# Four graph layers with GpSimd gathers: TensorE does a step's sum before its node stages

## The chip, the cores and the metric

The kernel runs on one core of one Trainium2 chip. The metric is the device time of one execution in microseconds. Three runs of the kernel before gave a median of 9930.19 us (9926.19 to 9943.86). One further execution, the profiled one, took 9929.83 us.

## What is computed

12,500 nodes with 64 features and 200,000 edges, sorted by their target node, go through four residual graph layers, each followed by a layer norm. The edges are the same in all. Cut to what matters:

```
x = layernorm(x + mlp_elu(x + segment_sum(x[src], dst)))
x = layernorm(x + mlp(concat(x, segment_sum(mlp(concat(x[src], x[dst], edge)), dst))))
h = l2norm(mean(x[src]) @ Wl1 + b1 + x @ Wr1);  h = relu(batchnorm(h))
x = layernorm(x + l2norm(l2norm(mean(h[src]) @ Wl2 + b2 + h @ Wr2) + x))
x = layernorm(x + segment_sum(x[src] @ Wrel[edge_type], dst))
```

## The kernel before, in words

The kernel makes five passes over the edges, numbered p = 0 to 4 and called **layers** here: the third reference layer needs two. Each pass gathers, for every edge, one row of a table in HBM (in_x, far_tab, x_tab, h_tab, rel_tab, lines 436 and following). All tables but the first are written by the pass before.

**Edges.** 128 edges are a chunk, 8 chunks a *step* (SUPERS = 196 steps a pass, indexed s). GpSimd issues one indirect DMA a chunk into G, which has 4 slots (s % 4); it may fill a slot again when `summed` says that the sum of step s - 4 is done. 200,000 edges are 1563 chunks (FILLED), so step 195 issues only 3. VectorE builds one-hot matrices OH of the targets (L748), TensorE multiplies each chunk's rows with them into PAG, a window of 96 nodes (`sum_straight`, `sum_window`, 8 matmuls, each of which stands as two records in the trace), and VectorE adds PAG to AGG (L779, `add_straight`). PAG is a single buffer: sum s waits for the add of sum s - 1. VectorE does the add of sum s - 1 in step s, ahead of its one-hot and its stages. In layer 1 the gathered rows are first added to PH, which TensorE computes for the next step (`pre_straight`), with a ReLU on ScalarE; in layer 3 VectorE *shifts* the gathered rows (L977) and ScalarE does the ReLU (L617) before the sum.

**Nodes.** 250 nodes are a *unit* (50 of them, 0 to 49). As soon as the sorted edges of a unit are summed, its dense part is done in four *stages*, 0 to 3 (node0 to node4 on each engine). `straight_schedule` fixes in which step each stage runs; SCHEDULE[s] lists them, mostly one stage in a step, and LATE holds those after the last step. At the end, SCHEDULE[192] is stage 3 of unit 47, 193 to 195 are stages 0, 1 and 2 of unit 48, and LATE is stage 3 of unit 48 and all of unit 49. Twice in a layer the schedule moves closer to the edges: step 104 holds stage 3 of unit 24 and stage 0 of unit 25, step 105 stages 1 and 2 of unit 25, and likewise steps 162 and 163 with units 39 and 40.

Stage 0 is ScalarE's fetch alone (Z, IU, XU, in layer 3 POS too; clearing AGG). What TensorE, VectorE (V) and ScalarE (S) do in the others:

| layer | stage 1 | stage 2 | stage 3 |
|---|---|---|---|
| 0 | T: NA, NB; V: NEG; S: exp; V: NEG | T: NB; V: layer norm (S: root) | T: transpose; S: XT; T: NA; S: STG, stores |
| 1 | T: transpose; S: XT | T: NA; S: POS | T: NB; V: layer norm; S: store |
| 2 | T: transpose; S: XT | T: NA, NB; S: Y; V: norm | T: transpose; S: store, HT; V: statistics |
| 3 | T: NB, NA; S: Y; V: norm | V: norm, layer norm (S: roots) | T: transpose; S: XT; T: PH, 4 products; S: STG, stores |
| 4 | T: transpose | V: layer norm | S: store |

Each engine has its own written-out program (`straight`), and each executes in order. ScalarE's and VectorE's programs for a step are, in this order: ScalarE its ReLU (layers 1 and 3), then its stages; VectorE the add of the last step, the mix or shift (layers 1 and 3), the one-hot for the next step, then its stages. The change touches TensorE's only. A second program (`turns`) is taken when the edge list is not regular enough; for these inputs the written-out one runs.

```
def gathers(p, s):
    ...
    if p == 1:
        pool.wait_ge(mixed, s + 1)
    else:
        pool.wait_ge(summed, SUPERS * p + s + 1)
```

```
if p == 3:
    pool.wait_ge(stored[2], all_stored(2))
```

The second fragment stands at the start of a pass on GpSimd (with its own number in each): no gather of a pass is issued before the last row of its table is stored.

Of the kernel before, what the change touches and what calls it, by code (L numbers as in the profile page):

```python
# [80 lines left out]
def gnn_kernel(nc, x, xT, src_c, dst_c, dst_r, type_c, efT, W1, b1, W2, b2, mW1, mb1, mW2T, mb2,  # L81
               uW1, ub1, uW2, ub2, Wl1, Wr1, sb1, gamma, beta, Wl2, Wr2, sb2, Wrel, out):
    ctx = ExitStack()
    with ctx:
# [253 lines left out]
        def slot_gathered(p, i):  # L338

            return i * (16 * GROUP) + 16 * GROUP * (TURNS * p + 1)  # L340
# [752 lines left out]
        def _(pe):  # L1093
            def mm(dst, lhsT, rhs, start=True, stop=True):
                return nc.tensor.matmul(dst, lhsT, rhs, start=start, stop=stop, skip_group_check=True)  # L1095
# [23 lines left out]
            def sum_window(p, h, m):  # L1119

                msg = HID[:, h % 2, :].rearrange("p (j c) -> p j c", j=GROUP) if p == 1 else G[:, h, :, :]
                for j in range(GROUP):
                    last = mm(PAG[0:m, 0:WIN], msg[:, j, 0:m], OH[:, h % 2, j, :], j == 0, j == GROUP - 1)
                return last
# [44 lines left out]
            def sum_straight(p, s, m):  # L1169

                h = s % SLOTS
                if p == 1:
                    pe.wait_ge(relu_done, s + 1)
                elif p == 3:
                    pe.wait_ge(bn_relu, s + 1)
                else:
                    if p == 0 and s == 0:
                        pe.wait_ge(onehot_ready, 1)
                    pe.wait_ge(added, SUPERS * p + s + 2)
                    pe.wait_ge(gathered[h], slot_gathered(p, s // SLOTS))  # L1180
                sum_window(p, h, m).then_inc(summed, 1)

            def pre_straight(t):

                b = t % 2
                pe.wait_ge(hotT_ready, t + 1)
                for j in range(GROUP):
                    c = slice(j * P, (j + 1) * P)
                    last = mm(PH[b][:, c], MIXT[:, b, c], MIXW[:, b, :], j % 4 == 0, j % 4 == 3)
                last.then_inc(pre_done, 1)  # L1190
# [63 lines left out]
            def batch_norm_row():  # L1254

                pe.wait_ge(bn_ready, 1)
                mm(NA[:, 0:H], BC[:, 2:3].to_broadcast([P, P]), IDENT[:, :]).then_inc(bn_rows, 1)
# [25 lines left out]
            def straight():  # L1283
                for p in range(LAYERS):
                    m = (D + 1, H, D, H, D)[p]
                    if p == 1:
                        pre_straight(0)
                    for s in range(SUPERS):
                        if p == 1 and s + 1 < SUPERS:
                            pre_straight(s + 1)  # L1290
                        for u, stage in SCHEDULE[s]:
                            node[p](u, stage)
                        sum_straight(p, s, m)
                    for u, stage in LATE:
                        node[p](u, stage)
                    if p == 2:
                        batch_norm_row()
# [21 lines left out]
            with pe.If(regular > 0):  # L1319
                straight()  # L1320
# [49 lines left out]
```

## Time and profile before

| | |
|---|---|
| median of the runs | 9930.19 us |
| the profiled execution | 9929.83 us |
| its span in the trace | 9928.0 us |
| GpSimd (POOL) busy | 7381.4 us, 74% |
| TensorE (PE) busy | 5057.8 us, 51% |
| VectorE (DVE) busy | 2602.1 us, 26% |
| ScalarE (ACT) busy | 1280.8 us, 13% |
| mean granted clock of TensorE | 0.583 |

The span runs from the first to the last instruction. An engine's busy time leaves out waits and the issuing of DMAs; the part of a gather that is issuing on GpSimd appears as "issue" beside it. The clock is a share of 2.4 GHz. In the timeline a row is one instruction, or several alike of one block, with its start and its length; the bracket names the idle time of the engine before it and what ended it.

### The profile page before, as it was taken

What the parts mean: (1) busy time and instruction counts of PE and PEld (TensorE: products, weight loads), DVE (VectorE), ACT (ScalarE), POOL (GpSimd) and SP (SyncE); (2) the same over time, 40 slices, a digit from 0 to 9 for tenths busy, and PEclk for the clock granted to TensorE, in tenths of its full rate; (3) what the DMA queues carried; (4) which work ended last, traced back from release to release, by engine and by line L of the source; (5) the groups of instructions that cost most, each with busy time, mean ns of one, the idle gap of its engine ahead of it and who ended that gap; (6) DMA issues with size and microseconds to landing.
All of it is one profiled execution on the core that took longest, in us unless ns stands there. A gap on an engine that the chain in (4) does not pass through costs nothing.

```text
span 9928.0 us, 68540 instructions
## 1 busy us (share of the span) xinstructions
PE 5057.8 (51%) x23622; PEld 4285.6 (43%) x23623; DVE 2602.1 (26%) x5963; ACT 1280.8 (13%) x2646; POOL 7381.4 (74%) x7823
## 2 busy tenths in 40 slices
PE   4555555566666666344444445666666633323333
PEld 3444444456666666333333334444555422222222
DVE  2222222233444443111111113333333311111111
ACT  1111111111111111000000001222222200000000
POOL 7777777767777777677777777777777667777777
PEclk6555555577777777555555555555555555555555
DMA  3111111133333333111111112222222211111111
GB/s 73 33 33 34 33 33 34 32 88 92 93 93 93 93 93 87 27 30 30 30 30 30 30 29 68 78 78 81 79 79 80 76 29 28 28 28 29 28 28 28
DMA packets 396618, 525.10 MB, mean 53 GB/s; under 512 B 175674, under 2 KB 232868, under 8 KB 396200
## 3 DMA queue, kind: packets, MB, share of 16 engines
q0 software_dynamic: 250080, 359.01, 16.0%
q1 hardware_dynamic: 56929, 81.63, 2.8%
q10 hardware_dynamic: 89255, 80.01, 2.6%
q8 instruction: 189, 3.10, 0.1%
q14 instruction: 165, 1.35, 0.0%
HBM read 442.81 MB, written 77.29 MB: 52 GB/s over the span
## 4 chain that ended last, share of the span: by engine, by line
POOL 74%; issue 25%; PE 1%; DVE 0%; DMA 0%; ACT 0%; ACTq 0%; POOLq 0%; DVEq 0%
POOL G L436 74%; PE PAG L1095 0%; PE NB L1095 0%; PE NA L1095 0%; PE PH L1095 0%; DMA G<-in_x,SRC 0%; DMA near_tab<-STG 0%; DVE FA L715 0%; DMA G<-rel_tab,IDX 0%; DMA h_tab<-STG 0%; ACT L503 0%; DMA G<-far_tab,SRC 0%; DMA G<-h_tab,SRC 0%; DVE HT L1031 0%; DMA G<-x_tab,SRC 0%
## 5 line engine op out<-in xcount | busy, mean ns | idle before, releaser
L1095 PE MATMUL PAG<-OH,G 128*64 128x96 f32 (+2 forms) x12544 | 2369.8, 383 | 3844.0 <-DMA G<-rel_tab,IDX 1370.1
L1095 PEld LDWEIGHTS PAG<-OH,G 128*64 128x64 f32 (+2 forms) x12544 | 2167.4, 253 | 4094.6 <-issue 3623.9
L436 POOL DMA_INDIRECT G<-rel_tab,IDX x1563 | 1474.7, 944 | 525.5 <-issue 525.5
L436 POOL DMA_INDIRECT G<-far_tab,SRC x1563 | 1474.9, 944 | 515.6 <-issue 476.1
L436 POOL DMA_INDIRECT G<-x_tab,SRC x1563 | 1475.5, 944 | 503.3 <-issue 476.0
L436 POOL DMA_INDIRECT G<-h_tab,SRC x1563 | 1475.0, 944 | 498.0 <-issue 475.7
L436 POOL DMA_INDIRECT G<-in_x,SRC x1563 | 1479.0, 946 | 476.1 <-issue 475.2
L779 DVE TENSOR_TENSOR AGG<-AGG,PAG 64x96 f32 (+2 forms) x980 | 245.6, 251 | 5510.9 <-PE PAG L1095 5501.0
L1095 PE MATMUL PAG<-OH,HT 128*128 128x96 f32 x3136 | 652.6, 393 | 630.2 <-ACT HT L614 630.2
L748 DVE TENSOR_TENSOR OH<-CONST,DREL 128x768 f32<-128x768 f32 x981 | 927.9, 946 | 3.7 <-issue 2.7
L1095 PEld LDWEIGHTS PAG<-OH,HT 128*128 128x128 f32 x3136 | 607.3, 297 | 678.0 <-ACT HT L614 677.6
L1095 PE MATMUL PH<-HT 128*128 128x128 f32 x3136 | 573.1, 359 | 17.9 <-DVE HT L817 17.8
L1095 PEld LDWEIGHTS PH<-HT 128*128 128x128 f32 x3136 | 558.1, 276 | 21.8 <-DVE HT L817 21.2
L1095 PE MATMUL PH<-wrel,XT 64*125 64x512 f32 x400 | 359.3, 1076 | 257.0 <-ACT XT L486 257.0
L1031 DVE TENSOR_TENSOR HT<-PH,G 128x1024 f32<-128x1024 f32 x196 | 240.0, 1225 | 753.5 <-DMA G<-far_tab,SRC 737.8
L614 ACT ACTIVATE HT<-HT 128x1024 f32<-128x1024 f32 x196 | 207.1, 1057 | 1608.7 <-DVE HT L1031 1608.7
L617 ACT ACTIVATE G<-G 128x1024 f32<-128x1024 f32 x196 | 207.1, 1056 | 1040.7 <-DVE G L977 1040.7
L977 DVE TENSOR_TENSOR G<-G,CONST 128x1024 f32<-128x1024 f32 x196 | 238.9, 1219 | 315.2 <-DMA G<-h_tab,SRC 314.4
L464 ACT ACTIVATE Z<-AGG 64x250 f32<-64x250 f32 (+2 forms) x250 | 101.5, 406 | 1686.2 <-DVE AGG L779 1610.4
L1095 PEld LDWEIGHTS PH<-wrel,XT 64*125 64x125 f32 x400 | 123.4, 323 | 433.3 <-ACT XT L486 276.1
L481 ACT ACTIVATE SQ<-VE 125x2 f32<-125x2 f32 x350 | 71.1, 203 | 1629.4 <-DVE VE L860 1457.1
L817 DVE SCALAR_TENSOR_TENSOR HT<-HT,FIRST,CONST 96x1024 f32<-96x1024 int16 x196 | 248.6, 1268 | 18.6 <-DMA HT<-near_tab 18.6
(151 smaller groups left out, 3840.1 us busy)
## 6 DMA issues: line engine op xcount, KB each, us to landing
rel_tab<-STG ACTq DMA_DIRECT2D x100, 500.0 KB
HT<-dst_rows SPq DMA_DIRECT2D x196, 192.0 KB
HT<-in_efT SPq DMA_DIRECT2D x196, 128.0 KB
G<-in_x,SRC POOLq DMA_INDIRECT x1563
G<-far_tab,SRC POOLq DMA_INDIRECT x1563
G<-x_tab,SRC POOLq DMA_INDIRECT x1563
G<-h_tab,SRC POOLq DMA_INDIRECT x1563
G<-rel_tab,IDX POOLq DMA_INDIRECT x1563
```

The lines of the kernel that those rows point to most:

```text
L436: pool.indirect_dma_start(out=G[:, h, j, 0:tabs[p].shape[1]], out_offset=None, in_=tabs[p], in_offset=bass.IndirectOffsetOnAxis(ap=numbers ...
L464: return nc.scalar.activation(dst, src_, ACT.Copy)
L481: nc.scalar.activation(SQ[0:HALF, :], VE[0:HALF, :], ACT.Sqrt).then_inc(root_ready[p], 1)
L614: nc.scalar.activation(HID[:, h % 2, :], HID[:, h % 2, :], ACT.Relu).then_inc(relu_done, 1)
L617: nc.scalar.activation(G[:, h, :, :], G[:, h, :, :], ACT.Relu).then_inc(bn_relu, 1)
L748: return nc.vector.tensor_tensor(OH[:, b, :, :], IOTA_P.unsqueeze(1).to_broadcast([P, GROUP, WIN]), d.unsqueeze(2).to_broadcast([P, GROUP, ...
L779: return nc.vector.tensor_tensor(dst, dst, PAG[0:m, 0:WIN], ALU.add)
L817: nc.vector.scalar_tensor_tensor(MIXT[0:WIN, b, :], DROW[:, b, :], FIRST[0:WIN, bass.ds(t, 1)], PIOTA_P[0:WIN, :].to_broadcast([WIN, SUPER ...
L977: nc.vector.tensor_tensor(rows_, rows_, CROW_P.unsqueeze(1).to_broadcast([P, GROUP, H]), ALU.add)\
L1031: nc.vector.tensor_tensor(HID[:, h % 2, :], PH[h % 2][:, :], G[:, h, :, :].rearrange("p j c -> p (j c)"), ALU.add)\
L1095: return nc.tensor.matmul(dst, lhsT, rhs, start=start, stop=stop, skip_group_check=True)
```

## The change

In TensorE's written-out program, the call that sums step s moves ahead of the loop over the stages of step s. Nothing else changes; the programs of VectorE, ScalarE, GpSimd and SyncE are the same instruction by instruction.

```diff
                     for s in range(SUPERS):
                         if p == 1 and s + 1 < SUPERS:
                             pre_straight(s + 1)
+                        sum_straight(p, s, m)
                         for u, stage in SCHEDULE[s]:
                             node[p](u, stage)
-                        sum_straight(p, s, m)
                     for u, stage in LATE:
                         node[p](u, stage)
```

TensorE at the end of layer 0, from stage 1 of unit 48. PAG is a sum, 8 matmuls a step; NA and the NB of ONES and Z are stage 1, the NB of w, NEG and rows stage 2, the NB of IDENT and XS opens stage 3. Before:

```order
L1095 MATMUL NA<-Z,w 128x250
L1095 MATMUL NB<-ONES,Z 125x1
L1095 MATMUL NA<-Z,w 128x250
L1095 MATMUL NB<-ONES,Z 125x1
L1095 MATMUL PAG<-OH,G 65x96 x8
L1095 MATMUL NB<-w,NEG 125x64 x2
L1095 MATMUL NB<-rows,ONES 125x64
L1095 MATMUL NB<-w,NEG 125x64 x2
L1095 MATMUL NB<-rows,ONES 125x64
L1095 MATMUL PAG<-OH,G 65x96 x8
L1095 MATMUL NB<-IDENT,XS 64x125 x2
```

and with the change:

```order
L1095 MATMUL PAG<-OH,G 65x96 x16
L1095 MATMUL NA<-Z,w 128x250
L1095 MATMUL NB<-ONES,Z 125x1
L1095 MATMUL NA<-Z,w 128x250
L1095 MATMUL NB<-ONES,Z 125x1
L1095 MATMUL PAG<-OH,G 65x96 x8
L1095 MATMUL NB<-w,NEG 125x64 x2
L1095 MATMUL NB<-rows,ONES 125x64
L1095 MATMUL NB<-w,NEG 125x64 x2
L1095 MATMUL NB<-rows,ONES 125x64
L1095 MATMUL NB<-IDENT,XS 64x125 x2
```

The sum of step 194 (the second half of the x16) now stands ahead of stage 1, and that of step 195 between stage 1 and stage 2 of the unit, where it stood behind stage 2.

TensorE in layer 3, from the sums before stage 3 of unit 47 to the opening of stage 3 of unit 48. NB of wl and the NA are stage 1, the NB of IDENT and PH are stage 3; stages 0 and 2 have nothing on TensorE. Before:

```order
L1095 MATMUL PAG<-OH,G 128x96 x16
L1095 MATMUL NB<-IDENT,XS 64x125 x2
L1095 MATMUL PH<-wrel,XT 125x512 x4
L1095 MATMUL PAG<-OH,G 128x96 x16
L1095 MATMUL NB<-wl,Z 125x64
L1095 MATMUL NA<-wr,POS 125x64
L1095 MATMUL NA<-rows,ONES 125x64
L1095 MATMUL NB<-wl,Z 125x64
L1095 MATMUL NA<-wr,POS 125x64
L1095 MATMUL NA<-rows,ONES 125x64
L1095 MATMUL PAG<-OH,G 128x96 x16
L1095 MATMUL NB<-IDENT,XS 64x125 x2
```

and with the change:

```order
L1095 MATMUL PAG<-OH,G 128x96 x16
L1095 MATMUL NB<-IDENT,XS 64x125 x2
L1095 MATMUL PH<-wrel,XT 125x512 x4
L1095 MATMUL PAG<-OH,G 128x96 x16
L1095 MATMUL NB<-wl,Z 125x64
L1095 MATMUL NA<-wr,POS 125x64
L1095 MATMUL NA<-rows,ONES 125x64
L1095 MATMUL NB<-wl,Z 125x64
L1095 MATMUL NA<-wr,POS 125x64
L1095 MATMUL NA<-rows,ONES 125x64
L1095 MATMUL PAG<-OH,G 128x96 x8
L1095 MATMUL NB<-IDENT,XS 64x125 x2
```

Before, the first x16 are steps 190 and 191; now they are 191 and 192, so that stage 3 of unit 47 follows the sum of step 192. Stage 1 of unit 48 follows the sum of step 194, which it preceded.

## Rows read from the trace of the kernel before

**Rows 1.** The page: chain that ended last by engine; one layer's gathers.
```profile
POOL 74%; issue 25%; PE 1%; DVE 0%; DMA 0%; ACT 0%; ACTq 0%; POOLq 0%; DVEq 0%
...
L436 POOL DMA_INDIRECT G<-h_tab,SRC x1563 | 1475.0, 944 | 498.0 <-issue 475.7
```

**Rows 2.** The waits of GpSimd (POOL): who for whom, us, times, longest.
```profile
POOL G L436 <- PE PAG L1095: 0.9, 3, 0.3
```

**Rows 3.** Timeline, end of layer 0: start, us, engine, line, operation, idle before.
```profile
1962.75 1.20 PE L1095 MATMUL NA<-Z,w 64*128 64x250 f32 x2
...
1966.12 0.86 DVE L891 TENSOR_SCALAR NEG<-NA,b1c 128x250 f32<-128x250 f32 x2 [2.05 <-PE NB L1095]
...
1969.85 0.68 DVE L903 SCALAR_TENSOR_TENSOR NEG<-NA,POS 128x500 f32<-128x500 f32 x1 [2.33 <-ACT NA L503]
...
1970.02 2.80 PE L1095 MATMUL PAG<-OH,G 128*65 128x96 f32 x16 [3.94 <-DMA G<-in_x,SRC]
...
1972.61 1.00 PE L1095 MATMUL NB<-w,NEG 128*125 128x64 f32 x4
...
1978.52 1.10 PE L1095 MATMUL NB<-IDENT,XS 125*64 125x125 f32 x4
```

**Rows 4.** Timeline, end of layer 1: stages 2 and 3 of unit 49.
```profile
3980.31 1.20 PE L1095 MATMUL NA<-XT,u 65*128 65x250 f32 x2 [0.47 <-ACT XT L486]
...
3982.91 0.68 PE L1095 MATMUL NB<-uw,POS 128*125 128x64 f32 x2 [0.56 <-ACT POS L523]
```

**Rows 5.** Timeline, end of layer 2.
```profile
5936.85 0.95 POOL L436 DMA_INDIRECT G<-x_tab,SRC  x1 [0.30 <-issue]
...
5939.40 2.79 PE L1095 MATMUL PAG<-OH,G 128*64 128x96 f32 x16 [6.35 <-DMA G<-x_tab,SRC]
5940.60 0.94 POOL L436 DMA_INDIRECT G<-x_tab,SRC  x1 [0.30 <-issue]
...
5942.12 0.79 PE L1095 MATMUL NA<-wl,Z 64*125 64x128 f32 x2
```

**Rows 6.** Timeline, end of layer 3: steps 193 to 195 and what follows.
```profile
7906.21 1.21 DVE L977 TENSOR_TENSOR G<-G,CONST 128x1024 f32<-128x1024 f32 x1
...
7907.45 1.06 ACT L617 ACTIVATE G<-G 128x1024 f32<-128x1024 f32 x1 [4.58 <-DVE G L977]
...
7908.56 3.73 PE L1095 MATMUL PAG<-OH,G 128*128 128x96 f32 x16 [2.66 <-ACT G L617]
...
7912.09 0.57 PE L1095 MATMUL NB<-wl,Z 128*125 128x64 f32 x2
...
7912.60 1.22 DVE L977 TENSOR_TENSOR G<-G,CONST 128x1024 f32<-128x1024 f32 x1
...
7915.35 0.52 ACT L557 ACTIVATE Y<-NB,IU 125x64 f32<-125x64 f32 x2 [0.45 <-PE NA L1095]
...
7917.51 0.48 DVE L984 SCALAR_TENSOR_TENSOR Y<-Y,RS,XU 125x64 f32<-125x64 f32 x2
...
7919.28 1.21 DVE L977 TENSOR_TENSOR G<-G,CONST 128x1024 f32<-128x1024 f32 x1
...
7921.28 0.28 DVE L876 TENSOR_TENSOR Y<-Y 125x128 f32<-125x128 f32 x1
...
7921.64 3.73 PE L1095 MATMUL PAG<-OH,G 128*128 128x96 f32 x16 [2.66 <-ACT G L617]
...
7925.30 1.09 PE L1095 MATMUL NB<-IDENT,XS 125*64 125x125 f32 x4
...
7926.92 7.18 PE L1095 MATMUL PH<-wrel,XT 64*125 64x512 f32 x8 [0.53 <-ACT XT L486]
...
7935.08 0.41 ACT L464 ACTIVATE Z<-AGG 128x250 f32<-128x250 f32 x1 [0.35 <-ACT STG L571]
...
7936.23 0.58 ACT L552 ACTIVATE POS<-HT,BSH,BSC 128x250 f32<-128x250 f32 x1
```

**Rows 7.** Windows, end of layer 3: us, busy PE, PEld, DVE, ACT, POOL; PEclk.
```profile
7913.60:7964.00 50.40, 28.90 (x75) 17.53 (x74) 14.02 (x51) 11.49 (x27) 0.94 (x1) 0.50 0.13 43
```

## The prediction

> **What bounds the kernel now.** I read the chain that ended last first: GpSimd's gathers hold 74% of the span and the "issue" time between them 25% [rows 1]. The group of one layer's 1563 gathers says how: 944 ns each and 475.7 us of issue gaps, so (1475.0 + 475.7) / 1563 = 1.248 us per gather and 9.985 us per step of eight. The reader is to see that 5 x 1563 x 1.248 us is 9.75 ms of the 9.93. Then the waits, for whether anything ever holds GpSimd up inside a layer: it waited for a sum (PAG) three times, 0.9 us in all [rows 2]. So TensorE has slack on every step but at a layer's end, where GpSimd may not gather until the last rows of a table are stored; there everything behind the last gather is on the path. Last, the timeline of those four ends and of single steps in layer 3.
>
> Step 195 has only 3 chunks, so its gather takes 3.7 us and not 10, and stage 2 of unit 48 is scheduled in step 195, stage 1 in 194. Those two stages now stand behind the sums of their steps.
>
> **The change, part by part.** No instruction is added or removed, no DMA is moved, and the other engines' orders are the same; TensorE alone exchanges about four blocks in each unit. What changes is who waits. Until now a stage's matmuls ran in the 6 or so us in which TensorE waited for gather s. Now they run after sum s, VectorE's part of the stage comes after them, and VectorE's add of sum s, for which sum s+1 waits (layer 3: the shift of gather s+1), is queued behind that part.
>
> *Layer 0's end* [rows 3]. Before, stage 1 of unit 48 ran at 1962.75, VectorE began on it 3.37 us later and finished at 1969.85 + 0.68, before it mattered. Sum 194 began at 1970.02, stage 2 at 1972.61, and the transpose that opens stage 3 at 1978.52. Now: sum 194 at 1970.02, stage 1 at 1972.6 (+2.6), VectorE at 1976.0 (+3.37), done at 1980.4 (+4.41, two ScalarE passes in it), the add of sum 194 and the handover 0.4 (chosen; adds of 0.25 us stand in all timelines), sum 195 at 1980.8, stage 2 at 1983.4, stage 3 at 1989.3 (the 5.91 us that lay between the two before). That is **+10.8 us**. The 5.91 holds a sum that now comes earlier, so 0.2 to 0.4 of it may go: 10.4 to 10.8.
>
> *Layer 1's end* [rows 4]. VectorE has work in stage 3 only. Stage 2's two products (NA) come behind sum 195 and ScalarE's pass after them is then in the open: from the NA matmul to the matmul of stage 3 it took 2.60 us for unit 49. **+2.6 us**.
>
> *Layer 2's end* [rows 5]. Before, stage 2 began at 5942.12, while the last gather (issued 5940.60) was still under way. A gather issued at 5936.85 let its sum start at 5939.40, 2.55 later; so sum 195 starts at 5943.15 and stage 2 a sum later (5942.12 - 5939.40 = 2.72), at 5945.9: **+3.8 us**.
>
> *Layer 4's end*: stage 2 has no TensorE work, and stage 1 of unit 48 fits between sums 194 and 195 while the last gather lands. **0**.
>
> *Layer 3* [rows 6] is the large one, as its steps were nearly full. In terms of VectorE's shift of a gather (L977), a plain step, shift to shift, takes 7912.60 - 7906.21 = 6.39 us with no gather to wait for: 2.35 to the sum, 4.04 from the sum. Stages 0 and 2 still cost no more than that, stage 2's VectorE part lying beside the sum. Stage 1 now takes 2.35 to the sum, 3.53 to its products (7912.09 - 7908.56), 3.26 until ScalarE's scaling (7915.35), 2.64 until VectorE ends (7917.51 + 0.48), 0.3 for the add and the shift: 12.1 us. Stage 3: 2.35, sum to transpose 3.66 (7925.30 - 7921.64), 1.62 to the PH products (7926.92), 8.16 until ScalarE is free (7935.08) and can do the ReLU of the next step; then 1.11 to the next sum and 4.04: 20.9 us for a stage-3 step and the stage-0 step behind it. A unit: 20.9 + 12.1 + 6.4 = 39.4 us, against 4 x 9.985 = 39.94 of gathers. It keeps up, by **0.5 us a unit**.
>
> At the end, without anything else, the pair before step 194 needs 20.93 us where the gathers give 19.97, so shift 194 is late by 1.0 us. Before it stood at 7912.60, a little late already; I move it to 7913.4 (chosen). Shift 195 comes 12.1 later, at 7925.5 instead of 7919.28: +6.2 us.
>
> But two steps of a layer hold two dependent stages (105 and 163: stages 1 and 2 of units 25 and 40). From the shift of the step before: ReLU at 15.8 + 1.7 for the unit's fetch on ScalarE (Z to POS, 7935.08 to 7936.81), sum 18.6, products 22.2, stage 1 done 28.1, stage 2 4.2 more (7921.28 to the transpose's 7925.30, and a gap), next shift 32.6. Two steps of gathers are 19.97: a backlog of 12.6 us each time. From step 106 to 162 are 14 units, which work off 7.3: 5.3 are left; the second jump makes 17.9 at step 164, the stage-3 pair adds 1.0, and 7 units until step 194 take off 3.6. Shift 194 is late by 15.2, not 1.0: +14.3. So layer 3 costs 6.2 + 14.3 = **+20.5 us**. Does GpSimd stall as well? Sum s frees its slot for the gather that would start 28.7 us after s landed (30 less 1.25); the sum behind a stage-3 step ends 10.8 us late on top of the 17.9, which is 28.7: at the very edge. A stall would only take from the later backlog what it costs, so the sum stands.
>
> In layers 0, 1 and 2 I leave no backlog at the end. Layer 0's steps are a sum of 2.6 us and, in the dearest one, stage 1 with 3.4 + 4.4 [rows 3], 11 us once in four steps; three cheaper steps of 10 us pay that back.
>
> **Sum.** 10.8 + 2.6 + 3.8 + 20.5 + 0 = 37.7 us on the profiled execution's 9929.83 gives 9967.5. The median of the runs shown is 9930.19, 0.4 above it, so I say **9967**.
>
> Bounds: the layer-3 term hangs on the 0.5 us a unit. At 1.0 the first backlog is gone by step 162, the second is 12.6 + 1.0 - 7 = 6.6 at step 194: layer 3 costs 12, the total is 29 (9959). At 0.2, 9.8 are left at step 162 and 22 at step 194: layer 3 costs 27, total 44 (9974). I take 0.5, since it is the sum of measured links.
>
> **Rivals.**
> *No backlog* (TensorE, once it has less waiting, or a shorter double step, lets layer 3 recover): only the ends count, 10.8 + 2.6 + 3.8 + 6.2 = 23.4: 9953. For it: 21 units recover over 0.5 us each only if my links add up to within 1%. Against: they are all from rows.
> *Layer 3 falls behind*: if a unit takes 41 us instead of 39.4, layer 3 becomes the bound of itself: 47 units x 1.1 = 50 and both jumps, 25, and 6: 81 in layer 3, 98 in all, 10028. The point is 39.94 us, only 1.4% above my 39.4. For it: small pauses in the chains. Against: the same links repeat to a few hundredths of a us in all units.
> *TensorE's clock makes up for it (not slower).* In the end of layer 3 the granted clock was 0.50, 1.2 GHz of 2.4, with 28.9 us of TensorE in 50.4 [rows 7]. The new order joins sums to stages in the four ends. If that brought full clock there, half of the TensorE time would go: 14 us in this end, and in the three others some 20 together (an estimate: they hold the same kinds of blocks, but no PH products), 34 in all, and 37.7 - 34 = 4: 9934, no change. It decides where TensorE runs most of these ends at 2.4 GHz; under 18 us saved it does not. Against it: this end has PH's four products and their weights in one run and stayed at 0.50. The Trainium skill (TensorE: Matmul & The Clock Gate, "Part 1: The HAM clock gate") says the clock rests at half rate and that sustained matmul activity releases it; by that rule these denser ends could be quicker, while the row at 0.50 speaks against it.
> *The moved waits don't reach the end*: if GpSimd's release did not hang on the last unit, 0. The stores' waits in all four layers speak against that.
>
> **Numbers.** A measurement of this kernel can tell about 0.2% (20 us) from no change. The forecast with its backlog (9959 to 9974) gets 0.55, no backlog 0.25, falling behind 0.12, the clock 0.04, the rest 0.04. The range 9950 to 9985 takes in the first two and the mild part of the third (a unit of up to about 40 us). No backlog lies 3 us above the 0.2% line at 9950, so a part of it falls within: faster 0.02, same 0.13, slower 0.85.
>
> **What would show it.** The gaps of GpSimd before layers 1, 2, 3 and 4 grow by 10.8, 2.6, 3.8 and 20.5 us. In layer 3 VectorE's shift stops waiting for the gather from step 106 on and finds it landed; the sums of layer 3 stop waiting for a fresh gather. GpSimd's waits for PAG stay under 3 us. Granted clocks stay as they were. I am wrong if layer 3's gap grows by 6 only, if GpSimd waits inside a layer by tens of us, or if layer 4's end moves.

## The result and the profile after

**The change makes the kernel slower by 0.3%.** The changed kernel took 9957.2 us in the median of 8 runs (9954.3 to 9965.2), the kernel before 9926.7 on the same chip: a ratio of 1.0030, 95% interval 1.0019 to 1.0041. The forecast was 9967, the range 9950 to 9985. The profiled executions stand at 9956.1 against 9929.8 us, spans 9954.3 against 9928.0: 26.3 us to explain.

The page of the kernel after, its chain by engine, then the gathers of layers 4, 1, 2, 3 and 0 (page, the columns as in [rows 1]):

```profile
POOL 70%; issue 24%; PE 3%; DVE 2%; ACT 1%; DMA 0%; DVEq 0%; ACTq 0%; POOLq 0%
...
L436 POOL DMA_INDIRECT G<-rel_tab,IDX x1563 | 1474.7, 944 | 538.2 <-issue 538.2
L436 POOL DMA_INDIRECT G<-far_tab,SRC x1563 | 1474.7, 944 | 526.0 <-issue 476.0
L436 POOL DMA_INDIRECT G<-x_tab,SRC x1563 | 1475.4, 944 | 505.8 <-issue 476.0
L436 POOL DMA_INDIRECT G<-h_tab,SRC x1563 | 1475.5, 944 | 499.3 <-issue 474.8
L436 POOL DMA_INDIRECT G<-in_x,SRC x1563 | 1479.1, 946 | 476.1 <-issue 475.8
```

The gathers are as long as before. PE and DVE have 3% and 2% of the chain, where they had 1% and 0%: the chain now runs back through part of layer 3. GpSimd's waits (who for whom: us in all, times, longest), before:

```profile
POOL G L436 <- issue: 2428.5, 7808, 49.4
POOL G L436 <- DMA near_tab<-STG: 39.5, 1, 39.5
POOL G L436 <- DMA x_tab<-XS: 27.3, 1, 27.3
POOL G L436 <- DMA h_tab<-STG: 22.0, 1, 22.0
```

and after:

```profile
POOL G L436 <- issue: 2440.8, 7807, 62.2
POOL G L436 <- DMA near_tab<-STG: 50.0, 1, 50.0
POOL G L436 <- DMA x_tab<-XS: 29.8, 1, 29.8
POOL G L436 <- DMA h_tab<-STG: 23.2, 1, 23.2
POOL G L436 <- PE PAG L1095: 1.5, 5, 0.3
```

The three DMA rows are the gaps ahead of layers 1, 2 and 3. The gap ahead of layer 4 is put down to "issue", as its longest. So the growth is 10.5, 2.5, 1.2 and 12.8 us, 27.0 in all, where 10.8, 2.6, 3.8 and 20.5 were forecast. All of the 26.3 us lies in these four gaps. The wait for PAG is 1.5 us [rows 2]; inside the layers GpSimd is hardly held up.

For layer 3, VectorE's waits from 6040 to 7990 us, the layer but for its first steps (same columns), before:

```profile
DVE AGG L779 <- PE PAG L1095: 841.7, 159, 29.8
DVE G L977 <- DMA G<-h_tab,SRC: 285.4, 102, 4.0
```

and after:

```profile
DVE AGG L779 <- PE PAG L1095: 712.2, 119, 12.5
DVE Y L990 <- ACT Y L557: 399.7, 50, 17.3
DVE G L977 <- DMA G<-h_tab,SRC: 64.8, 39, 5.5
```

The shift L977 waited for its gather 102 times, now 39 times. Taking from each shift's start that of the layer's first shift and s x 9.9877 us, a step of gathers, gives its **lateness**. Where layer 3 keeps up, it still swings within a unit: with the change, steps 147 to 151 stand at 0.4, 4.3, 6.5, 2.9 and 0.4, the 4.3 behind the stage-3 step. What exceeds that pattern is called backlog below. Between 163 and the end the pattern lies two steps further, with its 4.3 at steps 166, 170, ... 194 and 2.9 at 164, 168, ... 192.

| step | 104 | 106 | 120 | 124 | 132 | 162 | 164 | 168 | 188 | 190 | 194 | 195 |
|---|---|---|---|---|---|---|---|---|---|---|---|---|
| before | 0.0 | 3.7 | 0.1 | 0.2 | 0.2 | -0.2 | 4.0 | 0.0 | 0.1 | 0.2 | 0.2 | -3.1 |
| after | 4.2 | 16.4 | 16.3 | 12.3 | 7.5 | 2.5 | 15.2 | 15.1 | 14.7 | 11.8 | 11.9 | 14.1 |

### The profile page after: what moved, and what is told of

The parts are those of the page before. It is cut to its first block, busy times and chain, and to the rows that moved or that the text cites. A ratio compares the mean times of both kernels' runs of the same rounds, so it can differ in the third digit from the quotient of the medians.

```text
span 9954.3 us, 68540 instructions
## 1 busy us (share of the span) xinstructions
PE 4974.6 (50%) x23622; PEld 4222.8 (42%) x23623; DVE 2579.6 (26%) x5963; ACT 1297.9 (13%) x2646; POOL 7381.6 (74%) x7823
## 4 chain that ended last, share of the span: by engine, by line
POOL 70%; issue 24%; PE 3%; DVE 2%; ACT 1%; DMA 0%; DVEq 0%; ACTq 0%; POOLq 0%
POOL G L436 70%; PE PAG L1095 2%; PE PH L1095 1%; PE NA L1095 0%; PE NB L1095 0%; DVE G L977 0%; ACT G L617 0%; DMA G<-h_tab,SRC 0%; DVE Y L984 0%; DVE AGG L779 0%; ACT SQ L481 0%; DVE OH L748 0%; DVE XS L866 0%; DVE SS L877 0%; ACT Y L557 0%
## 5 line engine op out<-in xcount | busy, mean ns | idle before, releaser
L1095 PE MATMUL PAG<-OH,HT 128*128 128x96 f32 x3136 | 572.1, 358 | 502.9 <-ACT HT L614 502.9
L1095 PEld LDWEIGHTS PAG<-OH,HT 128*128 128x128 f32 x3136 | 541.1, 268 | 531.4 <-ACT HT L614 531.4
L1095 PE MATMUL PH<-HT 128*128 128x128 f32 x3136 | 533.2, 341 | 199.2 <-DVE HT L817 199.2
L1095 PEld LDWEIGHTS PH<-HT 128*128 128x128 f32 x3136 | 518.7, 256 | 214.2 <-DVE HT L817 207.9
L1095 PE MATMUL PH<-wrel,XT 64*125 64x512 f32 x400 | 320.9, 972 | 23.2 <-ACT XT L486 23.2
L486 ACT ACTIVATE XT<-NB 64x250 f32<-64x250 f32 (+1 forms) x200 | 74.7, 373 | 1541.5 <-PE NB L1095 1541.5
L977 DVE TENSOR_TENSOR G<-G,CONST 128x1024 f32<-128x1024 f32 x196 | 238.4, 1216 | 87.6 <-DMA G<-h_tab,SRC 87.0
```

What stands on the lines that cost most here:

```text
L486: nc.scalar.activation(XT[0:m, :], PT[0:m, :], ACT.Copy).then_inc(flip_copied[p], 1)
L977: nc.vector.tensor_tensor(rows_, rows_, CROW_P.unsqueeze(1).to_broadcast([P, GROUP, H]), ALU.add)\
```

## The experiments

In tails_only, steps_only, no_doubles and layer3_old_from_160 one condition in TensorE's written-out program decides for each step whether its sum stands first (the new order) or last:

```diff
-                        sum_straight(p, s, m)
+                        sum_first = ...
+                        if sum_first:
+                            sum_straight(p, s, m)
                         for u, stage in SCHEDULE[s]:
                             node[p](u, stage)
+                        if not sum_first:
+                            sum_straight(p, s, m)
```

### First set: ends and steps apart

tails_only has `s >= SUPERS - 2`: the new order in steps 194 and 195 of each layer alone.

> TensorE's new order in steps 194 and 195 of every layer alone; steps 0 to 193 as before. My theory (two costs: the ends of the layers, and in layer 3 a backlog from the steps before): GpSimd's gaps before layers 1 to 4 grow by 10.5, 2.5, 1 to 4 and 6 us (2 if TensorE's clock rises for the PH products there), 16 to 23 us slower than before in all. Rival 1 (all of the loss is made in the steps, the ends only show it): within 5 us of before. Rival 2 (only the ends matter and layer 3 has no backlog): as much as the whole change, 30 us.

steps_only has `s < SUPERS - 2`, the other half.

> The new order in steps 0 to 193 of every layer, steps 194 and 195 as before. My theory: gaps before layers 1, 2 and 3 as before (within 0.5 us); the gap before layer 4 grows by the backlog of layer 3, 8 to 15 us, and nothing else. Rival 1: about 30 us slower. Rival 2: within 3 us of before.

no_doubles has `p != 3 or not (103 <= s <= 106 or 162 <= s <= 164)`: the change, but with the old order around layer 3's two double steps.

> The whole change, but layer 3 keeps the old order in steps 103 to 106 and 162 to 164, around its two double steps. My theory: layer 3's shift stays under 7 us behind its gather everywhere, and the gap before layer 4 grows by 2 to 7 us over before instead of 12.8; the other gaps stay as in the changed kernel; 17 to 24 us slower than before. Rival (the backlog comes from every unit's stage 1 and 3, not from the double steps): the gap before layer 4 grows by 12 us or more again.

after_again is the changed kernel once more, one execution.

> The changed kernel once more, for TensorE's clock. If the two gaps that grew less than forecast (before layer 3 and before layer 4) owe it to a clock that happened to be at 2.4 GHz in their ends, they can be 2 to 8 us longer or shorter here, together with the lengths of their matmuls (PH products 7.2 or 3.7 us), while the gaps before layers 1 and 2 stay at 50 and 30. If the forecast's chains were wrong, the gaps repeat to a few tenths of a us.

GpSimd's gaps ahead of the layers, in us, and the times. The before of this set took 9935.2 us in the median of 23 runs.

| | layer 1 | 2 | 3 | 4 | span | time, runs | ratio to before |
|---|---|---|---|---|---|---|---|
| before | 39.5 | 27.3 | 22.0 | 49.4 | 9928.0 | | |
| the change | 50.0 | 29.8 | 23.2 | 62.2 | 9954.3 | | 1.0030 (own set) |
| after_again | 50.0 | 28.4 | 26.4 | 61.4 | 9964.6 | 9966.5, 1 | |
| tails_only | 49.9 | 29.8 | 23.2 | 51.4 | 9942.2 | 9955.1, 10 | 1.0022, 1.0012 to 1.0031 |
| steps_only | 37.1 | 27.3 | 22.0 | 65.7 | 9942.0 | 9943.0, 10 | 1.0008, 0.9999 to 1.0018 |
| no_doubles | 49.9 | 28.4 | 23.2 | 60.3 | 9952.3 | 9960.7, 8 | 1.0026, 1.0016 to 1.0037 |

*tails_only* has the first three gaps of the change, as expected, so these come from the last two steps alone. Ahead of layer 4 it has only 2.0 us: the 12.8 of the change are mostly no matter of the last two steps.

*steps_only* is the mirror of it: nothing ahead of layers 1 to 3 (layer 1's gap is even 2.4 us shorter: in layer 0's end the transpose and the products of stage 3 of unit 48 took 0.69 us each where before took 1.1 to 1.2, so TensorE's clock had risen there) and 16.3 us more ahead of layer 4. Its shift lateness is 15.3 at step 164, 15.6 at 188 and 16.5 at 194, against 0.2 before. What stands there when the last gather has landed is paid in full: 16.5 - 0.2 = 16.3. Of the 16.5, 4.3 are the pattern and 12 are backlog. It lies somewhat over what I expected. Its profiled span is 14.0 us longer, its timed ratio, 1.0008, takes in no change at all; only the gaps show it.

*no_doubles* was my miss. I had expected 2 to 7 us in layer 3's gap, as the jumps were out, and it grew by 10.9. Two things stand behind that. The old-order steps 162 to 164 left a little over 1 us of backlog, which was never worked off: lateness is 5.1, 5.0 and 4.9 us at steps 184, 188 and 192, 1.3 at 193, where a unit that recovers would be at 0. And even without it, shift 194 would be late by the pattern's 4.3, not by the 1.0 of my forecast; why, is told below, of late gathers. Shift 194 was late by 5.8 here; the end's own 6.2 us and 5.8 - 1.0 give 11.0.

*after_again* repeats the gaps of layers 1 and 4 within 1 us. Its span is 10.3 us longer than the first execution's, though the four gaps sum to 1.0 us more; its gathers were a little longer:

```profile
L436 POOL DMA_INDIRECT G<-rel_tab,IDX x1563 | 1476.4, 945 | 537.3 <-issue 537.3
L436 POOL DMA_INDIRECT G<-far_tab,SRC x1563 | 1476.7, 945 | 526.0 <-issue 476.0
L436 POOL DMA_INDIRECT G<-x_tab,SRC x1563 | 1476.8, 945 | 504.4 <-issue 475.9
L436 POOL DMA_INDIRECT G<-h_tab,SRC x1563 | 1477.4, 945 | 502.3 <-issue 473.2
L436 POOL DMA_INDIRECT G<-in_x,SRC x1563 | 1480.8, 947 | 476.0 <-issue 475.7
```

That is 1.4 to 2.0 us in each of five layers, 8.7 in all. One nanosecond a gather is 7.8 us a run, a quarter of the effect studied here. So gaps are compared below, and times only with the before of their own set.

### The recovery: where 0.5 us a unit goes

In the trace of the change, this is VectorE in the stage-2 step of unit 41, step 167 (timeline, columns as in [rows 3]):

```profile
7675.19 1.21 DVE L977 TENSOR_TENSOR G<-G,CONST 128x1024 f32<-128x1024 f32 x1
...
7681.11 0.23 DVE L838 TENSOR_SCALAR X<-XS 125x128 f32<-125x128 f32 x1
7681.77 0.26 DVE L779 TENSOR_TENSOR AGG<-AGG,PAG 128x96 f32 x1 [0.43 <-issue]
7681.94 1.21 DVE L977 TENSOR_TENSOR G<-G,CONST 128x1024 f32<-128x1024 f32 x1
```

Shift to shift it takes 6.75 us, not 6.39. Sum and stage are done, and VectorE spends 0.43 us on "issue" ahead of the add. There its program reads the window starts of the next four steps into registers, once in four steps. Before unit 25 and from unit 40 on, that read falls into the step behind stage 2 and lies open on the path; in units 25 to 39 the schedule has another phase, and those stage-2 steps take 6.39. In units 41 to 47 they took 6.60 to 7.10 us in each of the change, after_again and steps_only. The experiment, on the changed kernel, moves the read behind the one-hot, where VectorE has time:

```diff
-                        if h == 0:
-                            for k, w0 in enumerate(starts_of(dve, registers[s // SLOTS % 2], s)):
-                                starts[s + k] = w0
...
+                        if h == 0:
+                            for k, w0 in enumerate(starts_of(dve, registers[s // SLOTS % 2], s)):
+                                starts[s + k] = w0
```

It ran three times, twice in the disturbed sets told of below, then as load_later_3.

> load_later once more. The changed kernel's trace has since shown, in layer 3, 6.39 us from shift to shift for stage-2 steps of units 25 to 39, where the load is in another step, and 6.6 to 6.95 for units 40 to 47. Theory A: 6.39 to 6.5 us for all, the backlog from step 168 to 192 falls by 0.3 to 0.5 us a unit, the gap before layer 4 is 57 to 60 us, 2 to 4 us less than the changed kernel in all. Theory B (the later units' edges are slow for another reason): no difference to the changed kernel.

Time 9972.5 us (7 runs) against 9943.9 for its before (18 runs), 1.0028, interval 1.0017 to 1.0039. The same step in its trace:

```profile
7683.28 1.21 DVE L977 TENSOR_TENSOR G<-G,CONST 128x1024 f32<-128x1024 f32 x1
...
7689.16 0.23 DVE L838 TENSOR_SCALAR X<-XS 125x128 f32<-125x128 f32 x1
7689.51 0.26 DVE L779 TENSOR_TENSOR AGG<-AGG,PAG 128x96 f32 x1
7689.68 1.21 DVE L977 TENSOR_TENSOR G<-G,CONST 128x1024 f32<-128x1024 f32 x1
```

The 0.43 us are gone, the step takes 6.40. Lateness is 13.7, 13.2, 8.8, 8.5, 7.5, 7.0 and 6.5 at steps 168, 172, ... 192, so 0.3 to 1.0 less in a unit (and one jump of 4.4, told of below); with the change it is 15.1, 14.8, 14.7, 14.8, 14.8, 14.7 and 10.9, and but for the last jump, which is TensorE's clock again, it stays. From one shift to that of the next unit's same step, units with a jump left out, it is 39.48 us in three units here and 38.9 and 39.70 in two; in the change and in steps_only it is 39.70 to 40.30, mostly 39.84 to 39.99. The gathers of this run took 946 ns, so its gathers drift against the 9.9877 us a step: a shift that waited for its gather reads 3.3 at step 163 and 4.0 at step 193. That drift helps the recovery by 0.08 us a unit; the read, by some 0.4. Against the drift the backlog was all but gone at step 185, and shift 194 stood at 8.5 - 4.0 = 4.5. The read in the open step is what ate the recovery: it was moved in one undisturbed execution, and stood in the open in four (no_doubles too).

The gap ahead of layer 4 was 59.2 us, 9.8 over before's. That is the price of the change in layer 3 with no backlog and TensorE at 1.2 GHz: 6.2 and 4.5 - 1.0 = 3.5 are 9.7. The ratio, 1.0028 against 1.0030, doesn't tell the two kernels apart: this end's PH products took 7.19 us and those of the change 3.69, and with the transposes the clock gave the change back 4.0 us, half of its backlog of 7.6.

### Late gathers behind stage 3

My forecast had shift 194 late by 1.0. Here are unit 47's two stores of 500 KB in load_later_3, the last gather of step 194 and its shift:

```profile
7934.22 0.27 ACTq L574 DMA_DIRECT2D rel_tab<-STG  x1
...
7937.10 0.95 POOL L436 DMA_INDIRECT G<-h_tab,SRC  x1 [0.30 <-issue]
...
7937.63 0.27 ACTq L574 DMA_DIRECT2D rel_tab<-STG  x1
...
7944.13 1.22 DVE L977 TENSOR_TENSOR G<-G,CONST 128x1024 f32<-128x1024 f32 x1 [0.95 <-DMA G<-h_tab,SRC]
```

The shift waited for the gather itself, which landed 7.0 us after its last issue. In the trace of before the gathers of layer 3 with no such store issued from 9 us before their last issue to 3 us behind it landed 2.5 us after it on average and 3.0 at most; with one, 4.7 on average and up to 7.7. There the late one was the gather of step 193, which landed 6.2 us after its issue, with the stores at 7899.49 and 7902.90; shift 193 stood 3.8 late for it, and shift 194 did not. The new order does stage 3 after the sum, and the late gather becomes that of step 194. So where no backlog is left a shift behind stage 3 is still 3.7 us late or more; shifts 140, 144, 152 and 160 of the change waited 0.8 to 1.3 us for their gathers at a lateness of 4.1 to 5.1. That the stores are what delays the gathers is read from when both run; no run moved the stores alone.

### TensorE's clock in the ends

The rest of the miss lies in jumps of lateness by some 4 us: steps 124, 132 and 190 with the change. The granted clock there (windows, columns as in [rows 7]): an ordinary stretch, the stage-3 steps ahead of steps 124 and 190, and unit 47's and unit 48's stage 3:

```profile
7210.00:7222.00 12.00, 6.15 (x27) 5.62 (x26) 6.88 (x24) 2.18 (x6) 9.22 (x10) 0.50 0.21 55
7230.00:7239.00 9.00, 6.69 (x24) 4.39 (x24) 1.19 (x2) 5.10 (x11) 6.86 (x8) 0.85 0.36 99
7888.50:7897.50 9.00, 6.50 (x23) 4.20 (x24) 1.32 (x2) 5.30 (x11) 6.87 (x8) 0.87 0.33 100
7925.00:7933.00 8.00, 7.19 (x8) 2.48 (x8) 0.98 (x2) 2.42 (x5) 3.24 (x4) 0.50 0.25 67
7956.50:7963.00 6.50, 4.45 (x13) 1.80 (x12) 0.37 (x2) 3.31 (x8) 0.00 (x0) 0.99 0.10 28
```

and the PH products in them (timeline), at steps 123 and 189 and in unit 47's and unit 48's stage 3:

```profile
7230.22 3.69 PE L1095 MATMUL PH<-wrel,XT 64*125 64x512 f32 x8 [0.46 <-ACT XT L486]
...
7888.92 3.69 PE L1095 MATMUL PH<-wrel,XT 64*125 64x512 f32 x8 [0.46 <-ACT XT L486]
...
7925.08 7.19 PE L1095 MATMUL PH<-wrel,XT 64*125 64x512 f32 x8 [0.46 <-ACT XT L486]
...
7957.78 3.69 PE L1095 MATMUL PH<-wrel,XT 64*125 64x512 f32 x8 [0.53 <-ACT XT L486]
```

The fourth window is unit 47's, the fifth unit 48's. At times the clock stands at 2.4 GHz for a few us. Where that meets the four products they take 3.69 us for 7.19, ScalarE is free 3.5 us earlier, and the backlog, or the end itself, is that much shorter. In [rows 6] the same block took 7.18.

The rises under these products come with the new order. Of units 0 to 47 of layer 3 in five executions with the new order, the four products took 3.7 us in 10 units of the change, 10 of after_again, 8 of load_later_3, 8 of no_doubles and 5 of steps_only: 41 of 240. In before, tails_only and warm_ends_3, which keep the old order in those steps, they took 3.7 us in none of 144. What differs is what stands ahead of them: the step's sum, where in the old order TensorE had waited. That this neighbour is what raises the clock is argued and not tested: in [rows 6] the sum stands ahead too, and the block was slow. Which units are quick differs from execution to execution. A quick block does not always help: after those of steps 169 and 177 in no_doubles the next shift waited 2.9 and 3.7 us for its gather, which landed 8.5 and 8.1 us after its last issue.

In no_doubles and load_later_3 the end's block took 7.19, in after_again and tails_only 3.7. So tails_only's 2.0 us ahead of layer 4 are shift 195 later by 5.5 (12.2 us behind shift 194, 6.7 before), less 3.5. In layer 2's end it is alike. Sum 195 of the change, and after it that of after_again (timeline):

```profile
5956.45 1.50 PE L1095 MATMUL PAG<-OH,G 128*64 128x96 f32 x16 [0.47 <-DMA G<-x_tab,SRC]
```

```profile
5959.82 2.79 PE L1095 MATMUL PAG<-OH,G 128*64 128x96 f32 x16 [0.74 <-DMA G<-x_tab,SRC]
```

The first took 1.50 us, at a granted clock of 1.00; the second 2.79, at 0.50. With the slow one the gap grew by 4.4 us, with the fast one by 1.2. It was fast in tails_only, no_doubles and load_later_3 too, so in four of five executions.

Does the kernel before leave time there? warm_ends is the kernel before with added matmuls on constants in TensorE's idle stretches of the five ends; their result is never read.

```diff
+            def warm(n, bank=PH[0]):
+                for _ in range(n):
+                    mm(bank[:, P:2 * P], IDENT[:, :], IDENT[:, :])
...
+                        if s == SUPERS - 2:
+                            warm(AHEAD_OF_SUM[p])
...
+                        warm(AHEAD_OF_LATE.get((p, u, stage), 0), NB if (p, stage) == (3, 1) else PH[0])
```

AHEAD_OF_SUM is 6, 0, 8, 5 and 8 for the five layers; AHEAD_OF_LATE puts 1 to 14 ahead of ten of unit 49's stages. The undisturbed run is warm_ends_3.

> warm_ends once more, hoping for an undisturbed set (before near 9930 us). The two disturbed sets showed granted clocks of 0.55 to 0.76 in the ends, so TensorE's part of the ends shortens only partly: gaps before layers 1 to 4 of 35, 24, 20 and 47 us instead of 39.5, 27.3, 22.0 and 49.4, and 6 to 14 us less than before in all. If the fillers delay as much as the clock gives: within 3 us of before.

The clock in the ends rose from 0.50 to 0.65, 0.66, 0.57 and 0.57, and the gaps shrank by 4.2, 2.4, 1.0 and 0.1 us, 7.7 in all. Time 9938.6 us (11 runs) against 9943.9 (18), ratio 0.9994, interval 0.9985 to 1.0003: not to be told from no change. The first three gaps came near what was expected, the fourth hardly shrank. The end with the most TensorE work gained least. No kernel here is shown to beat the one before.

### Two disturbed sets

In two sets the kernel before itself took 11526.1 and 11506.6 us (13 runs each), 16% over its time elsewhere. Each set ran on a chip of its own, so what was special, the chip or the hour, can't be told. Three kernels ran in both: load_later, warm_ends and layer3_old_from_160. The last is the change with `p != 3 or s < 160 or s >= SUPERS - 2`, the old order from step 160 to 193 of layer 3.

> The changed kernel, with VectorE's load of four window starts (every fourth step, until now ahead of the add) moved behind that step's one-hot. Theory A (the load, 0.2 us on VectorE between stage 2's last instruction and the add, is what keeps layer 3 from working off its backlog in units 0 to 24 and 40 to 47): there a step with stage 2 takes 6.5 us from shift to shift instead of 6.75, the backlog from step 168 to 192 falls by 0.3 to 0.5 us a unit instead of 0.1, and the gap before layer 4 is 2 to 3 us shorter than a run of the changed kernel with the same clock, 57 to 60. Theory B (the stage-2 chain itself has become longer): 6.75 us again and the gap is 61 to 65. All other gaps as in the changed kernel.

> The changed kernel, but layer 3 keeps the old order in steps 160 to 193; steps 194 and 195 have the new one. If layer 3 loses by what it carries into its end, the backlog is gone by step 193 and the gap before layer 4 is 49.4 + 6.2 = 55.6 us, or 51.5 with the PH products at 2.4 GHz, as in tails_only, though the first double step stands in the new order. If steps before 160 matter, it is 3 us or more above that.

> The kernel before (old order everywhere), with matmuls on constants into a PSUM bank that nobody reads, in TensorE's idle stretches at the ends of the layers: 5 to 8 before sum 194, and 1 to 14 before stages of unit 49, sized to less than the idle time there. If TensorE's clock is what the shortened ends of the changed kernel owe their gain to, the granted clock in the ends rises from 0.50 towards 1.0, PH products take 3.7 us instead of 7.2, and the five ends together lose 15 to 30 us: 9900 to 9918. If the clock doesn't follow, the ends keep their length or grow by up to 3 us where a filler delays a stage.

> As load_later, whose set of runs was one in which the kernel before, too, took 11526 us. Theory A: a step with stage 2 takes 6.5 us from shift to shift in layer 3, the backlog from step 168 to 192 falls by 0.3 to 0.5 us a unit, and the gap before layer 4 is 57 to 60 us (less if TensorE's clock rises on the way). Theory B: 6.75 us and 61 to 65.

> As layer3_old_from_160, in an undisturbed set. If layer 3 loses by what it carries into its end: gap before layer 4 of 55.6 us, or 51.5 with the PH products at 2.4 GHz, though the first double step stands in the new order. If steps before 160 matter, 3 us or more above that.

> As warm_ends, in an undisturbed set: with TensorE's idle stretches at the layers' ends filled, the granted clock there rises from 0.50 towards 1.0 and the five ends together lose 15 to 30 us against before; if the clock doesn't follow, they keep their length or grow by up to 3 us.

Against the before of their own sets: load_later 11985.4, ratio 1.0401 (1.0384 to 1.0418), load_later_2 11920.6 (one run); layer3_old_from_160 11981.9 and 11973.9 (one run each); warm_ends 11523.3 and 11500.9, ratios 0.9999 (0.9989 to 1.0008) and 1.0000 (0.9990 to 1.0009). None of the numbers expected for an undisturbed run can be read here. The traces show engines waiting all through the run for signals labelled "remote", which the profile ties to no instruction or DMA of this kernel. In warm_ends (old order), GpSimd's wait and VectorE's:

```profile
DVE AGG L779 <- remote: 6285.8, 500, 39.3
...
POOL G L436 <- remote: 1155.7, 306, 7.7
```

The gathers of layer 0 there:

```profile
L436 POOL DMA_INDIRECT G<-in_x,SRC x1563 | 1478.6, 946 | 762.5 <-issue 444.0
```

and in load_later (new order):

```profile
L436 POOL DMA_INDIRECT G<-in_x,SRC x1563 | 1478.7, 946 | 884.7 <-issue 444.2
```

A gather is as long as ever, the idle time between them is 762 and 885 us, for 476 undisturbed. In these sets the two kernels that have the new order, wholly or but for part of layer 3, took 3.6 to 4.1% more than before, and not 0.3%; the changed kernel itself did not run in them. It would fit that each pause falls on a step whose slack the new order has used up, but no run tested that, and it stays an observation. layer3_old_from_160 ran in these two sets alone: whether the old order from step 160 on saves layer 3's backlog stays open.

## Why the prediction was right

The sign, the range and the mechanism held: the ends pay, and layer 3 carries a backlog into its end. Of 37.7 us forecast the profiled execution shows 26.3, the medians 30.5. That the sum came so near is partly luck: two terms were too small, and a clock that I had held fixed gave back more than both. By its steps:

- *Layer 0's end, +10.8*: found +10.5. The chain was, from the trace: sum 194 at 1970.40, stage 1 at 1973.13, VectorE 1976.50 to 1980.91, sum 195 at 1981.12, stage 2 at 1983.74, transpose at 1989.34. It took 18.94 us from sum 194 to the transpose, where [rows 3] have 8.50: +10.4. The handover chosen as 0.4 was 0.2.

```profile
1970.40 2.79 PE L1095 MATMUL PAG<-OH,G 128*65 128x96 f32 x16 [7.33 <-DMA G<-in_x,SRC]
...
1973.13 1.20 PE L1095 MATMUL NA<-Z,w 64*128 64x250 f32 x2
...
1980.23 0.68 DVE L903 SCALAR_TENSOR_TENSOR NEG<-NA,POS 128x500 f32<-128x500 f32 x1 [2.33 <-ACT NA L503]
...
1981.12 2.82 PE L1095 MATMUL PAG<-OH,G 128*65 128x96 f32 x16 [4.66 <-DVE AGG L779]
...
1989.34 1.09 PE L1095 MATMUL NB<-IDENT,XS 125*64 125x125 f32 x4 [2.38 <-DVE XS L866]
```

- *Layer 1's end, +2.6*: +2.5, and +1.1 in three other executions (in one of them, after_again, sum 195 took 2.42 us for 3.73).
- *Layer 2's end, +3.8*: right at 1.2 GHz (+4.4 in after_again), +1.2 where sum 195 and stage 2 ran at 2.4 GHz. I had taken the clock of [rows 5] as given.
- *Layer 4's end, 0*: there is no gap behind it to read; no growth beyond the four gaps is left over.
- *Both jumps, 12.6 each*: lateness rose by 12.2 from step 104 to 106 and by 12.7 from 162 to 164.
- *Stage 1's step, 12.1 us from shift 194 to shift 195*: 12.20.
- *Shift 194 late by 1.0 with no backlog*: **mis-sized.** It is 4.3 to 4.5, as load_later_3 and steps 148 to 160 of the change show. The pair before it does take 20.9 us, as I had it, in the change and in no_doubles; but the gather of step 194 now lands late, behind unit 47's stores, and I had put that at nothing ("no DMA is moved"). The stores stand in the same order, but at another time against the gathers. +3.5.
- *Recovery, 0.5 us a unit*: **mis-sized.** Stages 1 and 3 were sized right; the stage-2 step was taken as a plain 6.39 us, with stage 2's VectorE part "lying beside the sum", and is about 6.75 wherever VectorE's read of the window starts falls into it. In units 25 to 39, where it doesn't, recovery was 0.4 to 0.5; in units 41 to 46 about 0.1. The chain I read link by link in [rows 6] has no such read, and I counted only instructions with a row of their own. From step 164 to 188 that left 2.5 us more, 3.1 to the end.
- *Granted clocks stay as they were*: **wrong**, and larger than the other two, in the other direction. The new order itself brings the rises under the PH products: 41 quick blocks of 240 in the five executions that have it in the steps, none of 144 without. The rises at steps 124, 132 and 140 had the first backlog gone where 5.3 us were to be left, the one at step 190 took 4 us off, the one in the end 3.5.

The backlog at step 194 was thus 11.9 - 4.3 = 7.6 where 14.3 were forecast: 5.3 less from the first jump, 0.3 less in the second, 3.1 more by the recovery, 4.2 less by the clock. And layer 3 as a whole: 20.5 + 3.5 - 6.7 = 17.3 up to shift 195 (14.1 late where it had been 3.1 early, 17.2), less 4.0 from there to the first gather of layer 4 (40.73 us for 44.73: PH products 3.5, transposes 0.5) and 0.4 for the slightly slower gathers of this execution: 12.8. Without the clock's rises my sum would have been too small by some 6 us instead of too large by 8.
- *Rivals.* "No backlog" has the time nearest to the result (9953) and the wrong mechanism: a backlog of 12 us stands in layer 3 from step 164 to 188 and 7.6 to the end, and steps_only alone costs 16.3 us there. "Falls behind" did not come, but a unit with the exposed read takes about 39.85 us of the 39.94 that I had named as the point. "The clock makes up for it" was given 0.04 as a way to no change; as a part of the result it is true, and gave back over 10 us. In [rows 6] a sum, transposes and PH products stand nearly without a pause, and the clock stayed at 0.50; with the change it rose under such blocks in some units and did not stay up. The Trainium skill (TensorE: Matmul & The Clock Gate, "Part 1: The HAM clock gate") says that sustained activity raises the clock. The traces agree in that the denser order alone has the rises under these products, and disagree in that most such blocks (199 of 240) stayed slow.
- *The shift finds its gather landed from step 106 on*: so up to step 139 and from step 164; between, with the backlog gone, it waited again. 39 waits for 102 before. *GpSimd's waits for PAG under 3 us*: 1.5 with the change, 3.0 in after_again, 4.0 in load_later_3, the "very edge" of the forecast.

## What to carry to other kernels

When work is put behind a step's own input instead of in front of it, the steady state may hide it and the layer's end will not: price the last two steps of each stage by the rows, and ask of the busiest stage how much a dense step leaves behind and how fast it is worked off. A recovery of 1% a cycle is a difference of two large sums, so one open instruction of 0.4 us without a row of its own decides it: time whole cycles in the trace rather than adding links. And where a wait at the end depends on TensorE's clock, compare several executions before a few us are given a cause. Ask too which transfers a moved stage's stores will run beside.

## What the runs showed that I had not expected

- TensorE's granted clock goes to 2.4 GHz for a few us at a time within one layer and falls back, in other places in each execution of the same kernel; the same four products take 3.69 or 7.19 us, and 3.69 only where the step's sum stands ahead of them (41 of 240 blocks, 0 of 144 in the old order).
- A gather lands 2.5 us after its last issue, and 4.7 on average, up to 7.7, with a store of 500 KB near it (layer 3 of before).
- An engine's read of four values into its registers has no row in the timeline and costs some 0.4 us as "issue" where it lies open.
- The gathers' mean length differs between executions by 1 ns in 944, which is 8 us a run.
- For whole sets of runs engines waited for "remote" signals and the kernel before took 16% longer; kernels with the new order took 3.6 to 4.1% more than before in them.
